# ScalarE scales the normalised rows of the later groups of each layer, with a shift that VectorE makes

## The chip, the cores and the metric

The kernel runs on one core of one Trainium2 chip. The time is device microseconds of the run (median of several runs). The profile is one profiled execution with its own span.

## The reference

Four graph-attention layers over the same 4096 nodes with 64 features and one adjacency matrix. Layer l computes, with `slope` 0.2, 0.01, 0.2, 0.01 and an ELU in layers 0, 2 and 3 (layer 1 adds a bias instead):

```
wh = x @ W
e = leaky_relu((wh @ a_src)[:, None] + (wh @ a_dst)[None, :], slope)
p = softmax(where(adj > 0, e, -big), axis=1)
h = elu(p @ wh)            # layer 1: p @ wh + bias
r = x + h
x = (r - mean(r)) / sqrt(var(r) + 1e-5)     # over the 64 features of each row
```

The adjacency matrix is sparse, with few neighbours for nodes of a high number and many for those of a low one.

## The kernel before, in words

The 4096 rows are 32 tiles of 128 rows (`TILES`), and four tiles make a group (`GROUP`), so there are eight groups. In the first third of the kernel the adjacency matrix is read, and for each tile a list of its neighbours is made (`index`), while layer 0 begins. From then on a tile is worked on in its list form: GpSimd gathers the rows of `wh` of its neighbours from a table in HBM (`table`, one per layer) into `xg`, 128 slots at a time (`gather`, L525, 73 chunks per layer). Tile 0 alone is dense, against all 32 tiles of `wh`. A tile has one or more segments of up to 512 slots.

Each engine has one queue that is written out by hand: `run_round(l, i)` is called for one round after another, and a stage comes into the round that its lag says (`LAG_TILE`, in tiles). Layers 1 to 3 run one tile per round. The stages of a segment are: spread (TensorE, L667 and L669: scores into PSUM), slope (ScalarE, L840), mask (VectorE, L1221), exp (ScalarE, L854), turn (TensorE transposes, L686), copy_turned (ScalarE, L864), aggregate (TensorE, L701).

When a group's last tile is aggregated there follows the group's own part: combine (VectorE, L1238 to L1264, five rounds after the last tile's spread; ScalarE makes the exponential for the ELU, `elow`, L869), center (VectorE, `norm_stats`, one round later, and ScalarE's `estimate_rstd`, L811 and L813), scale (VectorE, `norm_rows`, one round later still), turn_x (TensorE, L561), copy_x (ScalarE, L805), project (TensorE, L571), copy_wh (ScalarE, L797), own (VectorE, L1212) and the write of the group's rows into the next layer's table (SP, L487, from `write_rows`; in the last layer the store, L491).

The order in ScalarE's round is: copy_turned, copy_x, slope, copy_wh, exp, rstd, elu. In VectorE's it is: mask, combine, scale, center, own. In TensorE's: project, turn, aggregate, turn_x, spread. Each engine works in the order of its queue, and waits at semaphores for the others: `x_made` counts groups whose rows are scaled, `rstd_made`, `masked`, `sloped`, `turned_copied` and so on.

The tensors of a group's end (`num`, `res`, `mean_var`, `stat`, `rstd`) have two halves, used in turn.

`GROUP_POS[l][g]` is the group's position in its layer's order. In layers 1 to 3 it is g. In layer 0 the tiles come in the order 0, 20 to 27, 1 to 19, 28 to 31, so the groups end in the order 5, 6, 0, 1, 2, 3, 4, 7. Groups 0 to 4 are the low ones: GpSimd starts the next layer's first 17 gathers (`EARLY`) when these five are written (`low_written`), and the other 56 when all are (`written`).

The rows are scaled in `norm_rows`: three small steps make `stat` (1/std), and then four instructions, one per tile, compute `x = (res - mean) * stat` (L1295), the last of which counts up `x_made`.

Of the kernel before, what the change touches and what calls it, by code (L numbers as in the profile page):

```python
# [24 lines left out]
P = 128  # L25
# [124 lines left out]
def group_n(l, g):  # L150

    return l * GROUPS + GROUP_POS[l][g]


def group_end(l, g):
# [104 lines left out]
def gat_kernel(nc, x_in, adj, adj_t, weights, bias, consts, out):  # L260
    with ExitStack() as ctx:
# [6 lines left out]
        def sem(name):  # L268
            return ctx.enter_context(nc.semaphore(name))
# [81 lines left out]
        stats = sb("stats", [P, GROUP, 6], F32)  # L351
        mean_var = sb("mean_var", [P, 2, GROUP, 2], F32)
        stat = sb("stat", [P, 2, GROUP], F32)
        var = sb("var", [P, 2, GROUP], F32)
        rstd = sb("rstd", [P, 2, GROUP], F32)

# [36 lines left out]
        flag_made = sem("flag_made")  # L393

        x_made = sem("x_made")
        xt_made = sem("xt_made")
        xt_copied = sem("xt_copied")
        wh_made = sem("wh_made")
# [61 lines left out]
        @block.sync  # L460
        def _(sp):
            sp.dma_start(wx[0:F, :, :], weights).then_inc(loaded, 16)
            sp.dma_start(wx[F:2 * F, :, :], weights).then_inc(loaded, 16)
            sp.dma_start(packed[:, :], consts["packed"]).then_inc(loaded, 16)
            sp.dma_start(fix_f[:, :], consts["fix"]).then_inc(loaded, 16)
            sp.dma_start(bit_mask[:, :], consts["bit_mask"]).then_inc(loaded, 16)
            for t, k in enumerate(TILE_AT):
                if t == 2:

                    sp.wait_ge(rows_marked, 1)  # L470
                if t >= 3:

                    sp.wait_ge(mask_made, t - 2)
                sp.dma_start(arena[:, t % 3, :], adj_t[k]).then_inc(adj_loaded[t % 3], 16)
                if t == 0:
                    sp.dma_start(arena[:, 2, :], adj[DENSE * P:(DENSE + 1) * P, :]).then_inc(rows_loaded, 16)
                    sp.dma_start(x[:, :, :], x_in).then_inc(x_loaded, 16)
                    sp.dma_start(slot_row[:, :], consts["slot_row"]).then_inc(slots_loaded, 16)
                    sp.dma_start(bias_sb[:, :], bias.rearrange("(o f) -> o f", o=1).broadcast_to([P, F])).then_inc(
                        slots_loaded, 16)  # L480

            def write_rows(l, g):

                n = group_n(l, g)
                if l < LAYERS - 1:
                    sp.wait_ge(wh_copied, GROUPS + n + 1)
                    sp.dma_start(tab_v[l + 1][:, g, :, :], wh[:, g * GROUP:(g + 1) * GROUP, :]).then_inc(  # L487
                        low_written if g < LOW_GROUPS else written, 16)
                else:
                    sp.wait_ge(x_made, n + 1)  # L490
                    sp.dma_start(out[:, g * GROUP:(g + 1) * GROUP, :],  # L491
                                 x[:, g * GROUP:(g + 1) * GROUP, :]).then_inc(stored, 16)

            for g in GROUP_ORDER[0]:
                write_rows(0, g)
            sp.wait_ge(flag_made, 1)
            over_flag = sp.value_load(flag[0:1, 0:1], min_val=0, max_val=1)
            with sp.If(over_flag == 0):
                for l in range(1, LAYERS):
                    for g in GROUP_ORDER[l]:  # L500
                        write_rows(l, g)
                sp.wait_ge(stored, 16 * GROUPS)
                sp.wait_ge(low_written, 16 * (LAYERS - 1) * LOW_GROUPS)
                sp.wait_ge(written, 16 * (1 + (LAYERS - 1) * (GROUPS - LOW_GROUPS)))
            with sp.Else():

                sp.wait_ge(xt_made, 2 * GROUPS)
                sp.wait_ge(x_made, GROUPS)
                sp.dma_start(x[:, :, :], x_in).then_inc(x_loaded, 16)
                for l in range(LAYERS):  # L510
                    with sp.Fori(0, TILES) as k:

                        sp.wait_ge(d_x, l * TILES + k + 1)
                        sp.dma_start(arena[:, 0, :], adj[bass.ts(k, P), :]).then_inc(d_adj, 16)
                sp.wait_ge(d_x, LAYERS * TILES + 1)
                sp.dma_start(out, x[:, :, :]).then_inc(stored, 16)
                sp.wait_ge(stored, 16)
                sp.wait_ge(low_written, 16 * LOW_GROUPS)
                sp.wait_ge(written, 16 * (1 + GROUPS - LOW_GROUPS))
# [33 lines left out]
        def _(pe):  # L553
# [152 lines left out]
            def run_round(l, i):  # L706

                g = group_of(l, "project", i)
                if g is not None and l < LAYERS - 1:
                    if GROUP_POS[l][g] == 0:  # L710
                        pe.wait_ge(sum_copied, l + 1)
                    project_rows(GROUPS + group_n(l, g), l + 1)
                for q in segs(l, "turn", i):
                    turn(l, q)
                for q in segs(l, "aggregate", i):
                    aggregate(l, q)
                g = group_of(l, "turn_x", i)
                if g is not None and l < LAYERS - 1:
                    if group_n(l, g) == 0:
                        pe.wait_ge(codes_read, LISTED)  # L720
                    pe.wait_ge(x_made, group_n(l, g) + 1)
                    turn_rows(GROUPS + group_n(l, g), g, xt_copied, GROUPS + group_n(l, g))
                for q in segs(l, "spread", i):
                    spread(l, q)
# [69 lines left out]
        def _(sc):  # L794
# [62 lines left out]
            def copy_turned(l, q):  # L857
# [5 lines left out]
                    sc.wait_ge(aggregated, n - ring + 1)  # L863
                nc.scalar.copy(slots(l, n)[:, 0:m * P], turned_ps[turned_bank(n)][:, 0:m * P]).then_inc(turned_copied, 1)  # L864

            def elu_part(l, g):
                h = GROUP_POS[l][g] % 2
                sc.wait_ge(agg_read, group_n(l, g) + 1)
                nc.scalar.activation(elow[:, h, :, :], num[:, h, :, :], ACT.Exp).then_inc(elow_made, 1)  # L869

            def run_round(l, i):
# [16 lines left out]
                g = group_of(l, "elu", i)  # L888
                if g is not None and ELU[l]:
                    elu_part(l, g)  # L890

            done_rounds = 0
            for t in range(BEATS):
# [52 lines left out]
        def _(v):  # L946
# [282 lines left out]
            def combine(l, g):  # L1229
# [25 lines left out]
                t.then_inc(agg_read, 1)  # L1255
                v.wait_ge(agg_read, group_n(l, g) + 1)
                xs = x[:, k0:k0 + GROUP, :]
                if l == BIAS_LAYER:
                    link(nc.vector.tensor_tensor(y, y, bias_sb[:, :].unsqueeze(1).broadcast_to([P, GROUP, F]), ALU.add))
                if ELU[l]:  # L1260
# [25 lines left out]
            def norm_rows(l, g):  # L1286
# [4 lines left out]
                link(nc.vector.tensor_tensor(st, r, r, ALU.mult))  # L1291
                link(nc.vector.tensor_tensor(st, st, var[:, h, :], ALU.mult))
                link(nc.vector.scalar_tensor_tensor(out=st, in0=st, scalar=1.5, in1=r, op0=ALU.add, op1=ALU.mult))
                for j in range(GROUP):
                    t = nc.vector.tensor_scalar(x[:, g * GROUP + j, :], res[:, h, j, :], mean_var[:, h, j, 0:1],  # L1295
                                                st[:, j:j + 1], ALU.subtract, ALU.mult)
# [211 lines left out]
```

## Time and profile before

| | |
|---|---|
| time of the runs (device us) | median 864.14 of 3 (862.48 to 875.75) |
| span of the profiled execution | 608.0 us, 10701 instructions |
| the rest of the time, outside the span | some 256 us of the median |
| mean granted TensorE clock | 0.922 |
| ScalarE busy | 398.5 us in 876 instructions |
| VectorE busy | 366.7 us in 1696 instructions |
| TensorE busy | 394.4 us in 3404 matmuls |

The span runs from the first instruction to the last of the profiled execution. The time of a run holds more than that span; no time of the profiled execution other than its span is given. The busy times are sums over the whole span; the share of an engine differs greatly between the list making (to about 250 us), the beginning of a layer and its end. Layers 1 to 3 take about 100 us each, from about 290 us on.

### The profile page before, as it was taken

To read this page: it belongs to the slowest core of one execution; us is meant where nothing else is said; L and a number is where in the kernel's file an instruction comes from. 1 tells how busy PE (TensorE), PEld (TensorE's weight loads), DVE (VectorE), ACT (ScalarE), POOL (GpSimd) and SP (SyncE) were. 2 spreads that over 40 slices of the span, in tenths; PEclk is the share of its full clock that TensorE was granted. 3 is DMA by queue.
4 is the path that set the end of the run, shared out by engine and by line. 5 is a ranking of instruction groups with operands and counts; after the bars stand their busy time and mean duration, and the time that the engine had idled before them with its cause. 6 is when DMAs were issued, how large, how long until landed. Compare 5 with 4: busy or idle time off the path is not lost.

```text
span 608.0 us, 10701 instructions
## 1 busy us (share of the span) xinstructions
PE 394.4 (65%) x3404; PEld 321.7 (53%) x3404; DVE 366.7 (60%) x1696; ACT 398.5 (66%) x876; POOL 282.3 (46%) x296
## 2 busy tenths in 40 slices
PE   2165454443788548886627997755898876498773
PEld 1154333332576436865416886543787754397552
DVE  2104579965327898898321289854168984218996
ACT  3377876857437776696328588727588863858882
POOL 0000035746024234400777777377777467777710
PEclk9999999999999999999566999959899986899995
DMA  7998999969348861200221122122222113122210
GB/s 300 388 428 333 392 425 403 406 240 295 143 185 273 295 240 15 38 19 26 35 27 27 28 37 46 42 45 30 28 28 46 36 38 46 27 29 37 45 34 25
DMA packets 20547, 84.86 MB, mean 140 GB/s; under 512 B 6083, under 2 KB 11462, under 8 KB 16262
## 3 DMA queue, kind: packets, MB, share of 16 engines
q1 hardware_dynamic: 10102, 73.14, 30.7%
q0 software_dynamic: 9344, 9.89, 12.1%
q10 hardware_dynamic: 1040, 1.08, 0.5%
q8 instruction: 30, 0.49, 0.3%
q14 instruction: 31, 0.25, 0.2%
HBM read 78.72 MB, written 5.37 MB: 138 GB/s over the span
## 4 chain that ended last, share of the span: by engine, by line
DVE 29%; PE 20%; ACT 11%; issue 5%; POOL 3%; DMA 1%; ACTq 0%; DVEq 0%
PE bank L701 9%; DVE num L1252 4%; PE bank L686 4%; DVE arena L1221 3%; DVE x L1295 3%; POOL xg L525 3%; PE bank L669 3%; ACT arena L854 3%; ACT arena L840 3%; DVE stats L1277 3%; DVE lone L1238 2%; PE bank L667 2%; DVE mean_var L1280 2%; ACT arena L864 1%; ACT arena L828 1%
## 5 line engine op out<-in xcount | busy, mean ns | idle before, releaser
L525 POOL DMA_INDIRECT xg<-table,index x292 | 282.1, 966 | 298.2 <-DMA table<-wh 134.9
L828 ACT ACTIVATE arena<-arena,half 128x4096 bf16<-128x4096 int32 x31 | 114.5, 3701 | 18.8 <-DMA arena<-in_adj_t 18.3
L1221 DVE CUSTOM_DVE_ANT_0 arena<-bank,arena 128x256 f32<-128x256 f32 (+3 forms) x123 | 62.8, 521 | 101.3 <-ACT arena L840 101.2
L840 ACT ACTIVATE arena<-bank,sloped_own 128x256 f32<-128x256 f32 (+3 forms) x123 | 67.9, 556 | 53.1 <-PE bank L669 52.1
L701 PE MATMUL bank<-xg,arena 128*128 128x64 f32 x486 | 72.6, 284 | 24.3 <-ACT arena L864 22.6
L701 PEld LDWEIGHTS bank<-xg,arena 128*128 128x128 f32 x486 | 63.6, 197 | 35.3 <-ACT arena L864 31.2
L686 PE MATMUL bank<-packed,arena 128*128 128x128 f32 x339 | 64.7, 312 | 19.1 <-ACT arena L864 16.5
L1018 DVE MAX8 top<-bank 128x8 f32<-128x256 f32 x31 | 13.3, 430 | 84.4 <-PE bank L603 84.3
L669 PE MATMUL bank<-packed,xg 128*128 128x128 f32 x324 | 63.3, 298 | 0.0
L686 PEld LDWEIGHTS bank<-packed,arena 128*128 128x128 f32 x339 | 43.2, 158 | 30.8 <-ACT arena L854 25.6
L864 ACT COPY arena<-bank 128x256 f32<-128x256 f32 (+3 forms) x123 | 53.6, 443 | 6.8 <-PE bank L686 6.2
L667 PE MATMUL bank<-off_row,wall 128*128 128x256 bf16 (+3 forms) x132 | 42.7, 324 | 22.0 <-DVE seg_max L1221 12.3
L854 ACT ACTIVATE arena<-arena,seg_max 128x256 f32<-128x256 f32 (+2 forms) x87 | 47.9, 551 | 4.9 <-DVE seg_max L1221 4.7
L669 PEld LDWEIGHTS bank<-packed,xg 128*128 128x128 f32 x324 | 45.4, 152 | 3.7 <-issue 1.4
L601 PE MATMUL bank<-fix,ones_b 3*128 3x352 bf16 x31 | 14.5, 468 | 45.8 <-ACT arena L828 45.8
L686 PE MATMUL bank<-packed,score 128*128 128x128 f32 x113 | 28.1, 370 | 20.9 <-ACT slots L864 20.4
L840 ACT ACTIVATE score<-bank,sloped_own 128x256 f32<-128x256 f32 (+3 forms) x41 | 22.7, 553 | 28.6 <-PE bank L669 28.4
L571 PE MATMUL bank<-wx_pair,xt 128*128 128x132 f32 x128 | 28.1, 355 | 13.5 <-ACT wh L797 10.1
L603 PEld LDWEIGHTS bank<-packer,arena 128*128 128x128 bf16 x992 | 28.8, 104 | 9.4 <-issue 9.4
L701 PE MATMUL bank<-xg,slots 128*128 128x64 f32 x162 | 28.9, 325 | 6.5 <-DVE num L1252 4.2
L1295 DVE TENSOR_SCALAR x<-res,mean_var,stat 128x64 f32<-128x64 f32 x128 | 32.2, 329 | 1.2
L667 PEld LDWEIGHTS bank<-off_row,wall 128*128 128x128 bf16 x132 | 19.0, 144 | 25.3 <-issue 14.5
(141 smaller groups left out, 765.3 us busy)
## 6 DMA issues: line engine op xcount, KB each, us to landing
arena<-in_adj_t SPq DMA_DIRECT2D x31, 2048.0 KB, 11.0
xg<-table,index POOLq DMA_INDIRECT x292, 2.7
table<-wh SPq DMA_DIRECT2D x24, 132.0 KB, 1.7
arena<-in_adj SPq DMA_DIRECT2D x1, 2048.0 KB, 12.9
table<-wh ACTq DMA_DIRECT2D x1, 1056.0 KB, 25.7
x<-in_x SPq DMA_DIRECT2D x1, 1024.0 KB, 15.0
out_x<-x SPq DMA_DIRECT2D x8, 128.0 KB
packed<-in_c_packed SPq DMA_DIRECT2D x1, 306.0 KB
```

Source lines behind the costliest of these rows:

```text
L525: pool.indirect_dma_start(out=xg[:, c, :], out_offset=None, in_=table[l][0:rows, :], in_offset=bass.IndirectOffsetOnAxis(ap=index[:, c:c + ...
L603: ins = nc.tensor.matmul(codes[:, c * w:(c + 1) * w], masks[:, t % 2, c * P:(c + 1) * P], packer[:, :], start=False, stop=(c == TILES - 1))
L667: nc.tensor.matmul(bank[:, 0:m * P], wall[:, :], marks, start=True, stop=False)
L669: t = nc.tensor.matmul(bank[:, c * P:(c + 1) * P], tcol_wide(terms[:, c1 + c, TCOL:TCOL + 1]), ident[:, :], start=False, stop=(c == m - 1) ...
L686: t = nc.tensor.transpose(turned_ps[turned_bank(n)][:, c * P:(c + 1) * P], scores(l, n)[:, c * P:(c + 1) * P], ident[:, :])
L701: t = nc.tensor.matmul(agg[:, at:at + F], slots(l, n)[:, c * P:(c + 1) * P], wh[:, c0 + c, 0:F] if k == DENSE else xg[:, FIRST[k] + c0 + c ...
L828: nc.scalar.activation(masks[:, t % 2, :], arena[:, t % 3, :], ACT.Sign, bias=half[:, :]).then_inc(mask_made, 1)
L840: nc.scalar.activation(scores(l, n)[:, 0:m * P], score_ps[n % len(score_ps)][:, 0:m * P], ACT.Relu, bias=sloped_own[:, k:k + 1], scale=ALP ...
L854: nc.scalar.activation(s, s, ACT.Exp, bias=least, scale=-1.0, accum_out=seg_sum[:, q:q + 1]).then_inc(exped, 1)
L864: nc.scalar.copy(slots(l, n)[:, 0:m * P], turned_ps[turned_bank(n)][:, 0:m * P]).then_inc(turned_copied, 1)
L1221: nc.vector.tensor_tensor_reduce(out=y, in0=score_ps[n % len(score_ps)][:, 0:m * P], in1=y, scale=-1.0, scalar=-FLOOR, op0=ALU.add, op1=AL ...
L1295: t = nc.vector.tensor_scalar(x[:, g * GROUP + j, :], res[:, h, j, :], mean_var[:, h, j, 0:1], st[:, j:j + 1], ALU.subtract, ALU.mult)
```

## The change

From position 3 on in layers 1 to 3 (five groups of eight) and from position 4 on in layer 0 (four groups), `norm_rows` on VectorE stops after `stat` and makes `shift = -mean * stat` (128x4) in one instruction, counted by `scale_made`. ScalarE then computes `x = Identity(stat * res + shift)`, four ACTIVATEs of 128x64 with scale and bias from columns of `stat` and `shift`, counted by `x_scaled`. It does so at the end of its round of stage "scale", behind that round's copy, slope and exp. TensorE's turn_x and SP's store wait for `x_scaled` in those groups. In combine, VectorE waits for ScalarE to have scaled the group two before, ahead of writing `res`. The other groups are unchanged.

```
+ACT_FROM = [4] + [3] * (LAYERS - 1)
+
+def on_act(l, g):
+    return GROUP_POS[l][g] >= ACT_FROM[l]
+
+def rows_made(l, g, on):
+    n = group_n(l, g) + 1
+    return sum(1 for m in range(LAYERS) for j in range(GROUPS) if group_n(m, j) < n and on_act(m, j) == on)
...
 # SP, write_rows, and TensorE, turn_x
-                    sp.wait_ge(x_made, n + 1)
+                    sp.wait_ge(x_scaled if on_act(l, g) else x_made, rows_made(l, g, on_act(l, g)))
...
-                    pe.wait_ge(x_made, group_n(l, g) + 1)
+                    pe.wait_ge(x_scaled if on_act(l, g) else x_made, rows_made(l, g, on_act(l, g)))
...
 # ScalarE
+            def scale_rows_of(l, g):
+                h = GROUP_POS[l][g] % 2
+                sc.wait_ge(scale_made, rows_made(l, g, True))
+                for j in range(GROUP):
+                    t = nc.scalar.activation(x[:, g * GROUP + j, :], res[:, h, j, :], ACT.Identity,
+                                             bias=shift[:, h, j:j + 1], scale=stat[:, h, j:j + 1])
+                t.then_inc(x_scaled, 1)
...
                 g = group_of(l, "elu", i)
                 if g is not None and ELU[l]:
                     elu_part(l, g)
+                g = group_of(l, "scale", i)
+                if g is not None and on_act(l, g):
+                    scale_rows_of(l, g)
...
 # VectorE, combine
                 xs = x[:, k0:k0 + GROUP, :]
+                n = group_n(l, g)
+                held = [m for m in range(max(0, n - 1)) if on_act(m // GROUPS, GROUP_ORDER[m // GROUPS][m % GROUPS])]
+                if held:
+                    v.wait_ge(x_scaled, len(held))
...
 # VectorE, norm_rows
                 link(nc.vector.scalar_tensor_tensor(out=st, in0=st, scalar=1.5, in1=r, op0=ALU.add, op1=ALU.mult))
+                if on_act(l, g):
+                    nc.vector.scalar_tensor_tensor(out=shift[:, h, :], in0=mean_var[:, h, :, 0], scalar=-1.0, in1=st,
+                                                   op0=ALU.mult, op1=ALU.mult).then_inc(scale_made, 1)
+                    return
                 for j in range(GROUP):
                     t = nc.vector.tensor_scalar(x[:, g * GROUP + j, :], res[:, h, j, :], mean_var[:, h, j, 0:1],
                                                 st[:, j:j + 1], ALU.subtract, ALU.mult)
```

The path for inputs that don't fit the lists (`Else`), which isn't taken here, waits for both counts.

## Rows read from the trace of the kernel before

**Rows 1.** The page, busy time, share of the span and instructions of each engine

```profile
PE 394.4 (65%) x3404; PEld 321.7 (53%) x3404; DVE 366.7 (60%) x1696; ACT 398.5 (66%) x876; POOL 282.3 (46%) x296
```

**Rows 2.** The chain of waits that ended last, by engine

```profile
DVE 29%; PE 20%; ACT 11%; issue 5%; POOL 3%; DMA 1%; ACTq 0%; DVEq 0%
```

**Rows 3.** Windows: one period, layer 2 (length, PE, PEld, DVE, ACT, POOL; clock; DMA)

```profile
482.70:489.60 6.90, 5.76 (x45) 4.44 (x44) 6.36 (x35) 6.05 (x24) 0.12 (x1) 1.00 0.06 20
```

**Rows 4.** Timeline of VectorE, layer 2, two scalings (start, us, engine, line, operation)

```profile
482.74 0.98 DVE L1295 TENSOR_SCALAR x<-res,mean_var,stat 128x64 f32<-128x64 f32 x4
...
483.71 0.42 DVE L1221 CUSTOM_DVE_ANT_0 arena<-bank,arena 128x256 f32<-128x256 f32 x1
...
484.05 0.42 DVE L1221 CUSTOM_DVE_ANT_0 arena<-bank,arena 128x256 f32<-128x256 f32 x1
...
484.40 0.42 DVE L1238 TENSOR_TENSOR lone<-sum_wh,lonely 128x256 f32<-128x256 f32 x1
...
489.62 0.54 DVE L1295 TENSOR_SCALAR x<-res,mean_var,stat 128x64 f32<-128x64 f32 x2
```

**Rows 5.** Timeline of ScalarE over the same scaling

```profile
482.27 0.48 ACT L840 ACTIVATE arena<-bank,sloped_own 128x256 f32<-128x256 f32 x1
482.64 0.51 ACT L854 ACTIVATE arena<-arena,seg_max 128x256 f32<-128x256 f32 x1
483.04 0.20 ACT L854 ACTIVATION_READ_ACCUMULATOR arena<-arena,seg_max 128x1 f32 x1
483.13 0.37 ACT L864 COPY arena<-bank 128x256 f32<-128x256 f32 x1
483.45 0.47 ACT L840 ACTIVATE arena<-bank,sloped_own 128x256 f32<-128x256 f32 x1
484.17 0.51 ACT L854 ACTIVATE arena<-arena,seg_max 128x256 f32<-128x256 f32 x1 [0.25 <-DVE seg_max L1221]
```

**Rows 6.** Groups by line and shape (count, busy us, mean ns; idle before)

```profile
L869 ACT ACTIVATE elow<-num 128x256 f32<-128x256 f32 x24 | 10.0, 416 | 9.4 <-DVE num L1252 9.3
L854 ACT ACTIVATE arena<-arena,seg_max 128x256 f32<-128x256 f32 x60 | 30.5, 508 | 4.7 <-DVE seg_max L1221 4.5
L854 ACT ACTIVATE arena<-arena,seg_max 128x512 f32<-128x512 f32 x9 | 6.4, 711 | 0.0
L816 ACT ACT_TABLE_LOAD x1 | 1.3, 1283 | 0.8 <-PEq L1497 0.8
...
L1293 DVE SCALAR_TENSOR_TENSOR stat<-stat,rstd 128x4 f32<-128x4 f32 x32 | 5.2, 163 | 1.1
```

**Rows 7.** Timelines of ScalarE, TensorE and VectorE, end of layer 2

```profile
495.90 0.63 ACT L864 COPY arena<-bank 128x256 f32<-128x256 f32 x2
...
496.30 1.97 PE L701 MATMUL bank<-xg,arena 128*128 128x64 f32 x8 [1.32 <-ACT arena L864]
...
504.53 0.69 PE L561 MATMUL bank<-packed,x 128*128 128x128 f32 x2 [4.02 <-DVE x L1295]
...
496.62 0.98 DVE L1295 TENSOR_SCALAR x<-res,mean_var,stat 128x64 f32<-128x64 f32 x4
...
498.31 0.47 DVE L1238 TENSOR_TENSOR lone<-sum_wh,lonely 128x256 f32<-128x256 f32 x1 [0.63 <-PE bank L701]
...
503.49 0.98 DVE L1295 TENSOR_SCALAR x<-res,mean_var,stat 128x64 f32<-128x64 f32 x4
```

**Rows 8.** Timelines of TensorE and VectorE, end of layer 0

```profile
283.88 1.10 PE L701 MATMUL bank<-xg,slots 128*128 128x64 f32 x8 [0.56 <-ACT slots L864]
...
284.20 0.98 DVE L1295 TENSOR_SCALAR x<-res,mean_var,stat 128x64 f32<-128x64 f32 x4
...
285.17 0.42 DVE L1238 TENSOR_TENSOR lone<-sum_wh,lonely 128x256 f32<-128x256 f32 x1
```

**Rows 9.** Waits of the whole span (us, times, longest), and GpSimd's timeline

```profile
POOL xg L525 <- issue: 85.9, 282, 0.3
...
489.48 0.94 POOL L525 DMA_INDIRECT xg<-table,index  x1 [9.48 <-DMA table<-wh]
```

More of the change, by code:

```diff
@@ L353, in gat_kernel @@
         stat = sb("stat", [P, 2, GROUP], F32)
+        shift = sb("shift", [P, 2, GROUP], F32)
         var = sb("var", [P, 2, GROUP], F32)
@@ L395, in gat_kernel @@
         x_made = sem("x_made")
+        scale_made = sem("scale_made")
+        x_scaled = sem("x_scaled")
         xt_made = sem("xt_made")
@@ L507, in _ @@
                 sp.wait_ge(xt_made, 2 * GROUPS)
-                sp.wait_ge(x_made, GROUPS)
+                sp.wait_ge(x_made, rows_made(0, GROUP_ORDER[0][-1], False))
+                sp.wait_ge(x_scaled, rows_made(0, GROUP_ORDER[0][-1], True))
                 sp.dma_start(x[:, :, :], x_in).then_inc(x_loaded, 16)
```

## The prediction

> **What bounds the kernel now.** I read four views, in this order. The page's engine totals: no engine passes 66% of the span [rows 1], so a total can't say what an engine's relief is worth. The chain of waits: VectorE has 29% of it, TensorE 20%, ScalarE 11% [rows 2]; it is a chain that hops between engines. Third, the windows over one group period (four tiles) late in a layer: in 6.9 us VectorE is busy for 6.36 and ScalarE for 6.05, TensorE for 5.76 at the full clock [rows 3]. Both engines that the change touches are nearly full there, and that is where the change acts. Fourth, the timelines of the two engines across one norm_rows, which decide.
>
> Number the groups p0 to p7 by their position in the layer's order. A group's combine, center and scale fall in rounds that I call A, B and C; the next one is D, and then the next group's A. In layer 2 the scaling of p4 starts at 482.74, that of p5 at 489.62: a period of 6.88 us [rows 4]. VectorE: three small statistics steps, four scalings (0.98 us together), the mask of D at 483.71, the mask of A at 484.05, the combine from 484.40, and from there to the next scaling there is no gap on it but some tenths around ScalarE's rstd. ScalarE: exponential of C until 483.13, copy of D at 483.13, slope of D 483.45 to 483.92, then it waits 0.25 us for a mask [rows 5]. The mask of A reads what the slope of D wrote. So VectorE and ScalarE turn in one loop: slope of D, mask of A, combine, statistics (VectorE), rstd (ScalarE), scaling (VectorE). Between the end of the slope of D (483.92) and the mask of A that uses it (484.05) there is a slack of 0.13 us, of which the hand-over needs about 0.03. That slack is all that ScalarE may lose there.
>
> **What the change does to that loop.** VectorE loses four scalings per moved group (0.98 us) and gains the shift, of the form of L1293, 163 ns [rows 6], with 0.03 us to the next: 0.79 us off VectorE. 19 groups move: p4 to p7 of layer 0, p3 to p7 of the other three. The shift ends at about 482.91, before ScalarE's queue is free at 483.13, so scale_made makes it wait for nothing in rounds with tiles. But the four ACTIVATEs stand at the end of round C, ahead of the copy, the slope and the exponential of D in ScalarE's queue. Call their time in that queue S. The slope of D ends at 483.92 + S, the mask of A starts at 483.95 + S instead of 484.05. TensorE's aggregate and turn_x wait for the same copy, its spread stands behind them in order; all shift by S together, none gets later than that. From the mask of A to the next scaling everything is as before, so the period grows by S - 0.10. The 0.79 us that VectorE saves are spent by it waiting for the slope of D.
>
> **The price S.** The trace has no ACTIVATE of 128x64 with a scale and a bias from columns. The nearest rows: 128x256 from SBUF without a column operand (elow) 416 ns, with a bias column (exponential) 508; 128x512 of the latter 711 [rows 6]. That is 0.80 ns per column of the tile and about 92 ns for the operand. At 64 columns: 508 - 192 x 0.80 = 354 ns with one column operand, and 446 with two if the second costs what the first did. Successive ACTIVATEs overlap by some 0.10 us (slope at 482.27 for 0.48, exponential at 482.64 [rows 5], which is 0.11), so 0.346 each and S = 1.38. Bounds: second operand free, 4 x 0.254 = 1.02; both free (elow's row), 4 x 0.162 = 0.65; no overlap, 4 x 0.446 = 1.78. I take 1.38, since the exponential's row differs from elow's by just such an operand; that its accumulated output costs the 92 ns in place of the column is the way to the lower values.
>
> The row of the exponential shows a bias column's price; the Trainium skill, in "ScalarE: Activation LUTs", section "What ACT_TABLE_LOAD costs", says that an ACTIVATE takes 186 ns + 0.833 per element, 93 more for each column operand, and that neighbours overlap by 93. The rows at 256 agree (416 and 508 against 399 and 492); no row here shows the second operand. An estimate by that page is S = 1.33. The same page's "Rules for kernel authors" would keep adds and multiplies on VectorE, which speaks against the change.
>
> **The sum, group by group.**
> - p3 to p5 of layers 1 to 3 and p4, p5 of layer 0, eleven groups: S - 0.10 each. The period is 6.8 to 7.0 us in all of them and the same loop stands in each.
> - p6. No tiles are left after it, but two copies stand behind its rstd, at 495.90, and now the scaling lies between them: the second copy can't start before 496.62 + 0.17 + 0.03 + S. It takes 0.36, then TensorE's last aggregate (half of eight matmuls in 1.97 us: 0.99), then p7's combine at 498.24 + S with hand-overs, against 498.31 [rows 7]: S - 0.07. So in layers 2 and 3. In layers 0 and 1 the eight take 1.10 and the combine starts right behind VectorE's scaling: 284.20 + 0.20 + S + 0.36 + 0.03 + 0.55 + 0.04 against 285.17 [rows 8]: S + 0.21. Together 4S + 0.28.
> - p7 of layers 1 to 3 has nothing behind it; its own latency counts. The shift takes the place of the scaling at 503.49, and TensorE's turn starts at 503.49 + 0.20 + S + 0.14 against 504.53 [rows 7]: S - 0.70. Three times: 3S - 2.10. In layer 3 the store stands for the turn. p7 of layer 0 is not on the path: what starts layer 1's tiles is GpSimd's early gathers, and they wait for the low groups alone, of which p6 is the last.
>
> Sum: 18S - 2.92 us. With S = 1.38 it is +21.9.
>
> **What costs nothing.** The wait for x_scaled ahead of res in combine is for the group two before, a whole period old; VectorE queues behind it, but it has passed. SP waits for x_scaled in layer 3 in place of x_made; only p7's store ends the kernel, counted above. The writes of layers 1 and 2 follow the copies of wh, later by what the groups are. GpSimd is the queue to check: its 17 early gathers of layer 3 start at 489.48 and, at 0.94 us and 0.30 of issue each [rows 9], end at about 510.6; the last write of layer 2 lands near 509 (an estimate: p7's turn at 504.53 [rows 7], and 4.7 us for its copy, projection, second copy and write). p3 and p4 delay the start by 2.6, all five delay the last write by 5.9 us; it would stand idle for some 1.8 us and be 4.4 late, less than those who use its rows. If that cover is gone, up to 2 us per layer come on top.
>
> Against the profiled execution: span 608.0 to 629.9 us. The time of the runs holds some 256 us around the span, which the change leaves alone; so 864.14 + 21.9 = 886.0.
>
> **The rivals.**
> 1. The ACTIVATEs are cheaper than their rows: S between 0.65 and 1.12. At S = 1.02 the sum is 15.4, 879.6 us; at 0.65 it is 8.8, 872.9. For it: the exponential also accumulates, which may be what the 92 ns buy. Against: its read of the accumulator is an instruction of its own [rows 5]. 2% is 17.3 us, which S = 1.12 gives; this is also about what a measurement can tell from no change.
> 2. The other side: the relief counts, since VectorE has no gap. ScalarE's own waits (0.25 us ahead of the exponential of D and the one ahead of rstd) would have to take the ACTIVATEs, which needs the slope of D to be early; then each of the eleven periods loses 0.79 us: -8.7, 855.4 us. It decides at the slack in the queue: S below 0.10, or a copy and slope of D that stand ahead of the scaling. The order of the queue and every row of ScalarE (none under 0.2 us) speak against it.
> 3. TensorE loses its clock. A new gap of S stands in every period. At the half level (1.2 GHz) the eight aggregates take 1.97 us instead of 1.10 [rows 7, 8]. With 5.76 us of matmuls per period [rows 3] it would be near 10.3, over the new period of 8.2: 2.1 us x 11 more, +23, 909 us. Against: the clock stood at 1.00 there, and the share of busy time falls only from 0.83 to 0.70.
> 4. Identity calls for another activation table. One load takes 1.28 us [rows 6], two per group, 19 groups: +49 on top, 935 us. For it: the kernel before uses no Identity in its trace. Against: copies, Relu, Sign, Exp and Ln run on one load. The Trainium skill, same page, "Table sets: the hidden batching unit", has identity in every set; no run shows it yet.
>
> **How the numbers follow.** Forecast (S 1.12 to 1.78): 0.57. Rival 1: 0.31. Rival 2: 0.05, rival 3: 0.04, rival 4: 0.01, and 0.02 for a gain that I don't see. The forecast's own range is 881 to 893, from 17.3 to 29.1 us. To hold 8 in 10 the range reaches down over most of rival 1, to 870, and up to 893. Slower by over 2%: 0.57 + 0.05, 0.62. Within 2%: rival 1 and most of rival 2, 0.35. Faster by over 2%: 0.03.
>
> **What would show it.** In the profile after: p4 to p5 of layer 2 at 8.2 us instead of 6.88; ScalarE's four ACTIVATEs at 0.35 us spacing right behind the exponential of C, and the slope of D behind them; VectorE idle for over a microsecond ahead of a mask, released by the slope, once per moved group; p0 to p2 unchanged. The forecast is wrong if the spacing is near 0.2, if the period stays at 6.9, or if VectorE's mask doesn't wait.

## The result and the profile after

The changed kernel takes 884.22 us (median of 5 runs, 878.45 to 897.81), the kernel before 862.48 beside it (5 runs, 859.62 to 875.75). The ratio is 1.0237, 95% interval 1.0188 to 1.0286; it leaves out the runs that lie over 1.5% above their kernel's fastest, which are the two near 897 us and the one of 875.75. So the change makes the kernel slower, and whether by more than 2% isn't decided. A warning on that interval: the kernel before, run against itself in a later job (run 1 below), gave 1.0094, interval 1.0019 to 1.0169. A few runs of this kernel can mislead by 1%. Its median was 876.99, 875.66 and 873.41 us in the three later jobs, where it is 862.48 here, and the changed kernel was timed in this one job only. So the readings below come from the traces wherever they can, and the ratios only frame them.

The page of the changed kernel, its span and totals:

```profile
span 876.6 us, 10746 instructions
PE 424.6 (48%) x3404; PEld 347.7 (40%) x3404; DVE 353.4 (40%) x1639; ACT 425.0 (48%) x952; POOL 277.0 (32%) x296
```

Against [rows 1] VectorE has lost 57 instructions (76 scalings gone, 19 shifts come) and 13 us, and ScalarE has gained 76 instructions and 26.5 us. But the span is 876.6 us, where 608.0 and a cost of some 20 would give about 630. Some 256 us that no row of the first profile shows are inside the execution here. Run 1 shows that this is so in the kernel before too: a timed run is only about 1.9 us longer than its own span, and the execution of 608.0 us was of another kind than the timed ones. So run 1's trace, and not that of the 608.0 us execution, is what the trace after has to be read against.

The four ACTIVATEs by their line (count, least/median/greatest ns):

```profile
L890 ACT ACTIVATE x<-res,shift,stat x76: 424/431/442, 305.4 to 873.5; 128x64 f32<-128x64 f32 x76
```

ScalarE's timeline over the scaling of p4 in layer 2, and the next one (start, us; the numbers answer to [rows 5]):

```profile
669.23 0.20 ACT L873 ACTIVATION_READ_ACCUMULATOR arena<-arena,seg_max 128x1 f32 x1
669.32 1.43 ACT L890 ACTIVATE x<-res,shift,stat 128x64 f32<-128x64 f32 x4
670.65 0.35 ACT L883 COPY arena<-bank 128x256 f32<-128x256 f32 x1
670.90 0.47 ACT L859 ACTIVATE arena<-bank,sloped_own 128x256 f32<-128x256 f32 x1
...
677.37 0.76 ACT L890 ACTIVATE x<-res,shift,stat 128x64 f32<-128x64 f32 x2
```

VectorE over the same stretch (it answers to [rows 4]):

```profile
668.93 0.16 DVE L1330 SCALAR_TENSOR_TENSOR shift<-mean_var,stat 128x4 f32<-128x4 f32 x1
669.01 0.16 DVE L1243 TENSOR_SCALAR sloped_own<-wh 128x4 f32<-128x4 f32 x1
669.08 0.42 DVE L1252 CUSTOM_DVE_ANT_0 arena<-bank,arena 128x256 f32<-128x256 f32 x1
...
671.41 0.42 DVE L1252 CUSTOM_DVE_ANT_0 arena<-bank,arena 128x256 f32<-128x256 f32 x1 [1.90 <-ACT arena L859]
671.76 0.42 DVE L1269 TENSOR_TENSOR lone<-sum_wh,lonely 128x256 f32<-128x256 f32 x1
```

Read the two together. ScalarE starts the scaling at 669.32, right behind the exponential of round C; the copy of D comes 1.33 us later, the slope of D ends at 671.37, and VectorE's mask of A starts at 671.41, after 1.90 us of idleness that the slope ends. Before, that mask stood back to back with the one ahead of it. The period from this scaling to the next is 8.05 us, where [rows 4] have 6.88 and the prediction had 8.2.

The same stretch by windows (length; PE, PEld, DVE, ACT, POOL busy; granted clock; DMA), and one of layer 3:

```profile
669.40:677.40 8.00, 5.52 (x41) 4.47 (x40) 5.58 (x32) 7.22 (x28) 0.54 (x1) 0.97 0.05 18
...
839.10:847.60 8.50, 7.13 (x36) 6.35 (x34) 5.63 (x32) 6.82 (x25) 0.00 (x0) 0.60 0.04 15
```

VectorE's 6.36 us of [rows 3] are 5.58, as it should be, in a longer period. In layer 3 TensorE's granted clock is 0.60, between its levels of 2.4 and 1.2 GHz (a mix of both in the window), where the kernel before has 1.00; these periods take 8.5 us instead of 8.05. The clock falls at about 840.7, where TensorE takes up work after the second of two idle gaps, 1.12 us (to 838.33) and 1.13 (to 840.77). A gap of over a microsecond is no sign by itself: run 1 has one of 1.12 us per period in layer 3 at 1.00, and the window of layer 2 above has one of 1.14 at 0.97.

### The profile page after: what moved, and what is told of

The parts are those of the page before. It is cut to its first block, busy times and chain, and to the rows that moved or that the text cites. A ratio compares the mean times of both kernels' runs of the same rounds, so it can differ in the third digit from the quotient of the medians.

```text
span 876.6 us, 10746 instructions
## 1 busy us (share of the span) xinstructions
PE 424.6 (48%) x3404; PEld 347.7 (40%) x3404; DVE 353.4 (40%) x1639; ACT 425.0 (48%) x952; POOL 277.0 (32%) x296
## 2 busy tenths in 40 slices
DMA packets 20548, 84.86 MB, mean 97 GB/s; under 512 B 6084, under 2 KB 11463, under 8 KB 16263
## 4 chain that ended last, share of the span: by engine, by line
another core or an unknown queue 19%; PE 17%; DVE 14%; ACT 13%; issue 11%; ACTq 0%; DVEq 0%
PE bank L720 7%; ACT arena L873 3%; PE bank L688 3%; PE bank L705 3%; ACT x L890 3%; ACT arena L859 2%; DVE num L1283 2%; ACT arena L883 2%; PE bank L686 2%; DVE stats L1312 2%; DVE arena L1252 1%; DVE lone L1269 1%; DVE mean_var L1315 1%; ACT arena L847 1%
## 5 line engine op out<-in xcount | busy, mean ns | idle before, releaser
L544 POOL DMA_INDIRECT xg<-table,index x292 | 276.8, 948 | 506.5 <-DMA table<-wh 306.4
L705 PE MATMUL bank<-packed,arena 128*128 128x128 f32 x339 | 71.5, 334 | 115.0 <-issue 80.1
L720 PE MATMUL bank<-xg,arena 128*128 128x64 f32 x486 | 80.5, 304 | 47.0 <-ACT arena L883 42.7
L705 PEld LDWEIGHTS bank<-packed,arena 128*128 128x128 f32 x339 | 49.6, 173 | 124.5 <-issue 103.4
L720 PEld LDWEIGHTS bank<-xg,arena 128*128 128x128 f32 x486 | 71.9, 219 | 59.4 <-ACT arena L883 53.7
L686 PE MATMUL bank<-off_row,wall 128*128 128x256 bf16 (+3 forms) x132 | 46.2, 350 | 81.5 <-issue 70.8
L688 PE MATMUL bank<-packed,xg 128*128 128x128 f32 x324 | 70.2, 322 | 0.0
L688 PEld LDWEIGHTS bank<-packed,xg 128*128 128x128 f32 x324 | 50.2, 166 | 4.6 <-issue 2.3
L622 PE MATMUL bank<-packer,arena 128*128 128x11 bf16 x992 | 34.4, 173 | 16.0 <-issue 16.0
L622 PEld LDWEIGHTS bank<-packer,arena 128*128 128x128 bf16 x992 | 30.3, 105 | 26.1 <-issue 26.0
L686 PE MATMUL bank<-off_dense,wall 128*128 128x512 bf16 x32 | 16.8, 526 | 39.9 <-DVE seg_max L1252 22.2
```

The source lines that it names most:

```text
L544: pool.indirect_dma_start(out=xg[:, c, :], out_offset=None, in_=table[l][0:rows, :], in_offset=bass.IndirectOffsetOnAxis(ap=index[:, c:c + ...
L622: ins = nc.tensor.matmul(codes[:, c * w:(c + 1) * w], masks[:, t % 2, c * P:(c + 1) * P], packer[:, :], start=False, stop=(c == TILES - 1))
L686: nc.tensor.matmul(bank[:, 0:m * P], wall[:, :], marks, start=True, stop=False)
L688: t = nc.tensor.matmul(bank[:, c * P:(c + 1) * P], tcol_wide(terms[:, c1 + c, TCOL:TCOL + 1]), ident[:, :], start=False, stop=(c == m - 1) ...
L705: t = nc.tensor.transpose(turned_ps[turned_bank(n)][:, c * P:(c + 1) * P], scores(l, n)[:, c * P:(c + 1) * P], ident[:, :])
L720: t = nc.tensor.matmul(agg[:, at:at + F], slots(l, n)[:, c * P:(c + 1) * P], wh[:, c0 + c, 0:F] if k == DENSE else xg[:, FIRST[k] + c0 + c ...
```

## The experiments

Ten runs follow; run 1 is the kernel before, the other nine have an edit each. S is the time that the four scalings take in ScalarE's queue; rounds A to D and groups p0 to p7 are those of the prediction. A "stretch" below is the time from the end of p3's scaling in layer 0 to the end of p7's in layer 3, from the starts of L1295 and L890 (or their like) and their lengths in one profile. It leaves out the list making at the start, whose length differs by some 25 us from run to run. Where a period is said to be "by the statistics", it goes from the start of VectorE's last statistics step (`stat<-stat,rstd`, L1293 or its like) of one group to that of the next. This step stands in every group of every kernel, while the scaling itself starts later once it is moved.

**1. The kernel before, once more.** No edit.

> The kernel before, once more, for its profile in the state in which the timed runs are. The profile shown ahead of the prediction has a span of 608.0 us where the runs take 862; the profile of the changed kernel has 876.6 of 878.5. Theory A (the missing 256 us are stretches inside the execution in which engines stand idle, the same in both kernels): span about 860, idle stretches at the ends and beginnings of layers 1 to 3, late group periods of 6.9 us as in the first profile. Theory B (they lie outside the span in the kernel before and the change brought the stretches in): span near 608 again.

Measured: span 883.7 us. Theory A holds. Of the 275.7 us between the two spans, 218 lie in the stretch and 45 ahead of layer 0's first scaling. Behind layer 0, ScalarE, VectorE and TensorE stand idle together for over 2 us at a time once in the 608.0 us execution (7.8 us), and 27 times here, 182 us in all. The idle stretches stand where the timeline of GpSimd shows gathers one behind the other. In layer 1's dense part (ScalarE, VectorE and TensorE, with GpSimd's row):

```profile
388.63 0.94 POOL L525 DMA_INDIRECT xg<-table,index  x1 [0.30 <-issue]
...
390.43 0.69 ACT L840 ACTIVATE arena<-bank,sloped_own 128x512 f32<-128x512 f32 x1 [13.31 <-remote]
391.15 0.69 DVE L1221 CUSTOM_DVE_ANT_0 arena<-bank,arena 128x512 f32<-128x512 f32 x1 [13.30 <-ACT arena L840]
...
392.38 1.06 PE L669 MATMUL bank<-packed,wh 128*128 128x128 f32 x4
...
404.43 0.69 ACT L840 ACTIVATE arena<-bank,sloped_own 128x512 f32<-128x512 f32 x1 [13.31 <-remote]
```

TensorE is done at 393.44 and ScalarE's slope of its scores starts at 404.43. In the 11.0 us between, no engine but GpSimd has an instruction; where GpSimd is quiet such a hand-over takes about 0.03. The late periods are as in the first profile. A window of layer 2:

```profile
676.50:683.40 6.90, 5.76 (x45) 4.45 (x45) 6.38 (x35) 6.05 (x23) 0.00 (x0) 1.00 0.06 20
```

**7 and 8. Both kernels without the gathers of layers 1 to 3.** One gather per layer is left, and the layers compute with the rows of layer 0.

```
-                    for c in EARLY:
-                        gather(l, TILES_OF_CHUNK[c][0], c, LOW * P)
...
-                    for c in range(NCH):
-                        if c not in EARLY:
-                            gather(l, TILES_OF_CHUNK[c][0], c)
+                    gather(l, 1, FIRST[1])
...
-                    pe.wait_ge(gathered[k], 16 * OWN[k] * (l + 1))
+                    pe.wait_ge(gathered[k], 16 * (OWN[k] + (l if k == 1 else 0)))
```

> The kernel before with one gather in each of layers 1 to 3 in place of 73: the rows gathered in layer 0 are used again, so these layers compute something else; all the rest of the work is the same. Theory A (the idle stretches of 5 to 13 us come with GpSimd's gathers, since they lie exactly where GpSimd is busy): they are gone from the layers 1 to 3, and the time falls from 862 to about 600. Rival (they have another cause, such as the code after the branch being fetched): they stay, over 800 us.

> The changed kernel with the same cut. If theory A holds there is no idle stretch to hide behind in layers 1 to 3, and the whole sum should show against the kernel before with the cut: 18 x 1.33 - 2.92 = 21 us, of which layer 0 has 4, each of the others 5.6. Rival (the sum overrates p6 and p7 by itself, not because of the idle stretches): 14 us.

Measured: medians 640.97 us (before) and 668.02 (changed), four runs each; the fastest runs 629.61 and 657.13, 27.5 apart. The idle stretches are gone from layers 1 to 3 (theory A; those that are left lie in the list making, with layer 0's gathers). The stretch is 329.7 us in the one and 357.1 in the other, so the change costs 27.3 us when nothing hides it: 6.9 in layer 0, 7.7, 6.1 and 6.7 in the others. That is more than the 21 of the sum. The rest goes with a lower clock, as in the windows of the two kernels over p4 of layer 1, changed kernel first:

```profile
423.50:431.80 8.30, 6.88 (x42) 6.04 (x42) 5.57 (x33) 7.20 (x27) 0.00 (x0) 0.79 0.06 19
```

```profile
414.50:421.40 6.90, 5.69 (x45) 4.49 (x45) 6.38 (x35) 5.82 (x22) 0.00 (x0) 1.00 0.07 22
```

and in two periods of run 8 by the statistics, p3 to p4 of layer 1 and of layer 2:

```profile
413.57:422.43 8.86, 7.73 (x41) 7.31 (x42) 5.71 (x31) 6.99 (x25) 0.00 (x0) 0.61 0.04 14
521.19:529.24 8.05, 5.56 (x43) 4.48 (x44) 5.63 (x32) 7.27 (x27) 0.00 (x0) 1.00 0.06 19
```

The granted clock parts these periods. The changed kernel and runs 5 and 8 have 29 periods behind a moved inner group that no idle stretch falls into. In ten of them the clock stands at 0.97 or 1.00, and each of the ten takes 8.04 or 8.05 us, within 0.07 of the prediction's rule. In the other 19 the clock is between 0.50 and 0.80, and they take 8.22 to 9.10. In run 9 below (shorter scalings, 7.68 us at the full clock) two periods are long at 1.00 and 0.98, 8.09 and 8.13 us; both follow directly on one with a lowered clock (0.80 and 0.62). In run 8 the seven of that kind are 4.6 us over 8.05 together, which is most of the 6.3 that the sum lacks; p6 is 1.6 over its terms. Without the change (the first profile, runs 1 and 7) 28 of the 31 such periods have 0.96 or more.

**2. The same four ACTIVATEs behind the slope of round D.**

```
                 for q in segs(l, "slope", i):
                     slope(l, q)
+                g = group_of(l, "scale", i - 1)
+                if g is not None and on_act(l, g):
+                    scale_rows_of(l, g)
...
-                g = group_of(l, "scale", i)
-                if g is not None and on_act(l, g):
-                    scale_rows_of(l, g)
```

> The same four ACTIVATEs, moved in ScalarE's queue from the end of round C to behind the copy and the slope of round D; nothing else changes. Queue theory (they cost because the slope of D, and with it VectorE's mask of A, stands behind them): the mask of A is not delayed any more; what remains is ScalarE's own fullness, 6.05 us + 1.33 of work in a period, so late periods of about 7.4 in layers with an ELU (6.9 in layer 1) in place of 8.05 to 8.25; in all some 12 to 15 us less than the changed kernel, ratio to before 1.005 to 1.01. Rival (what costs is that ScalarE has more work at all, or the longer hand-over VectorE to ScalarE to TensorE): periods stay above 8, ratio 1.02.

Measured: ratio 1.0139 (1.0009 to 1.0269), stretch 569.2 us against 575.2 of the changed kernel and 559.3 of the kernel before. ScalarE, layer 2, p5:

```profile
683.37 0.37 ACT L883 COPY arena<-bank 128x256 f32<-128x256 f32 x1
683.69 0.47 ACT L859 ACTIVATE arena<-bank,sloped_own 128x256 f32<-128x256 f32 x1
684.06 1.42 ACT L890 ACTIVATE x<-res,shift,stat 128x64 f32<-128x64 f32 x4
685.39 0.50 ACT L873 ACTIVATE arena<-arena,seg_max 128x256 f32<-128x256 f32 x1
```

and VectorE's mask of A:

```profile
684.20 0.42 DVE L1252 CUSTOM_DVE_ANT_0 arena<-bank,arena 128x256 f32<-128x256 f32 x1 [0.59 <-ACT arena L859]
```

The mask starts 0.04 us behind the slope, under the scalings instead of behind them. Layer 1, which has no ELU, has periods of 6.84 and 6.83 us, no more than before; in layers 2 and 3 p4 to p5 takes 7.67 and 7.44. By the statistics, which don't move with the scaling, the periods behind moved inner groups are 7.67 and 7.68 in layer 0, 6.83 twice in layer 1, 8.45 and 8.13 in layer 2, and 7.32, 8.08 and 7.45 in layer 3. The longest two of layers 2 and 3 stand at a clock of 0.63 (8.45) and 0.50 (8.08); the 8.13 follows the first of them. Where there is no ELU the queue theory is right: the order alone takes 1.2 us per period away, with the same work on ScalarE. In the layers with an ELU it takes 0.4 to 1.4 us away in layers 0 and 3 and nothing in layer 2, where the periods were 8.24 and 8.04, so there the rival, that ScalarE has more work at all, isn't refuted. The total fell by 6 us in the stretch, less than the 12 to 15 expected; the ratio, whose interval is wide, can't decide between its two expectations.

**3. The scalings made twice** (first into a spare tile).

```
+                for j in range(GROUP):
+                    nc.scalar.activation(spare[:, j, :], res[:, h, j, :], ACT.Identity,
+                                         bias=shift[:, h, j:j + 1], scale=stat[:, h, j:j + 1])
                 for j in range(GROUP):
                     t = nc.scalar.activation(x[:, g * GROUP + j, :], res[:, h, j, :], ACT.Identity,
```

> ScalarE makes each of the four scalings twice, once into a spare tile that nobody reads. S goes from 1.33 to 2.66 us per group. Queue theory by the sum 18 S - 2.92: 45 us over before in place of 21, so 24 us more than the changed kernel, ratio to before about 1.052; late periods of 9.4 to 9.6 us. Rival (ScalarE's time is partly covered): less than 12 us more.

Measured: ratio 1.0634 (1.0434 to 1.0834), stretch 604.6 us, 45.3 over the kernel before, against 45.0 by the sum. One period of layer 1, p4 to p5 (ScalarE):

```profile
512.65 1.43 ACT L894 ACTIVATE x<-res,shift,stat 128x64 f32<-128x64 f32 x4
520.70 1.43 ACT L891 ACTIVATE spare<-res,shift,stat 128x64 f32<-128x64 f32 x4
522.02 1.43 ACT L894 ACTIVATE x<-res,shift,stat 128x64 f32<-128x64 f32 x4
```

It is 9.37 us, so nothing of ScalarE's second 1.33 us was covered. That the whole stretch meets the sum so closely is partly chance: 5.0 us of the 45.3 lie between p7 of layer 0 and p0 of layer 1, where the other profiles with idle stretches differ by 3.9 us among themselves (130.3 to 134.2), whatever the edit.

**4. Plain copies in place of the scalings.** The normalisation of the moved groups is left out.

```
-                    t = nc.scalar.activation(x[:, g * GROUP + j, :], res[:, h, j, :], ACT.Identity,
-                                             bias=shift[:, h, j:j + 1], scale=stat[:, h, j:j + 1])
+                    t = nc.scalar.copy(x[:, g * GROUP + j, :], res[:, h, j, :])
```

> ScalarE copies the four tiles of res to x without scale and shift: the normalisation of the moved groups is left out, with all waits and the same four instructions in number and size. It takes both column operands away. By the row of elow 0.26 us each, 0.16 apart, S = 0.65: sum 8.8 us over before, ratio 1.010, late periods of 7.4 us. Rival (the hand-over, not S, is what costs): as the changed kernel, 1.02.

**9. The shift from its column, the scale a constant.** The division by the deviation is left out in the moved groups.

```
                     t = nc.scalar.activation(x[:, g * GROUP + j, :], res[:, h, j, :], ACT.Identity,
-                                             bias=shift[:, h, j:j + 1], scale=stat[:, h, j:j + 1])
+                                             bias=shift[:, h, j:j + 1], scale=1.0)
```

> The changed kernel with the shift from its column but a scale of 1.0 as a constant, so the moved groups are not divided by their deviation. It prices the second column operand. If each column operand costs about 92 ns, as the prediction took it: 0.34 us each where the changed kernel has 0.43, 0.24 apart, S = 0.98, late periods of 6.88 + 0.98 - 0.10 = 7.76 us at the full clock. Rival (the second operand is free): 0.43 us and 8.05 as in the changed kernel.

Measured, the forms of the two (mean ns), plain copies first:

```profile
L890 ACT COPY x<-res 128x64 f32<-128x64 f32 x76 | 12.8, 242 | 4.6 <-DVE shift L1329 4.4 <-issue 0.2
```

```profile
L890 ACT ACTIVATE x<-res,shift 128x64 f32<-128x64 f32 x76 | 20.1, 337 | 5.0 <-DVE shift L1330 4.4 <-issue 0.6
```

So 242, 337 and 431 ns for no, one and two column operands: each costs 94 to 95 ns, the second like the first, and they start 0.144, 0.24 and 0.333 us apart. Four such starts make S = 0.58, 0.96 and 1.33. The periods p4 to p5 of layer 1 follow them; from the starts, the copies first and then the one column:

```profile
509.61 0.67 ACT L890 COPY x<-res 128x64 f32<-128x64 f32 x4
516.93 0.67 ACT L890 COPY x<-res 128x64 f32<-128x64 f32 x4
```

```profile
510.49 1.05 ACT L890 ACTIVATE x<-res,shift 128x64 f32<-128x64 f32 x4
518.17 1.05 ACT L890 ACTIVATE x<-res,shift 128x64 f32<-128x64 f32 x4
```

| | S | period of layer 1, p4 to p5 | 6.88 + S - 0.10 | eleven periods over run 1 | 11 S - 0.76 | stretch over run 1 | 18 S - 2.92 |
|---|---|---|---|---|---|---|---|
| plain copies | 0.58 | 7.32 | 7.36 | 8.4 | 5.6 | 5.9 | 7.5 |
| one column | 0.96 | 7.68 | 7.74 | 13.7 | 9.8 | 15.3 | 14.4 |
| changed kernel | 1.33 | 8.05 | 8.11 | 17.0 | 13.9 | 15.9 | 21.0 |
| scaled twice | 2.66 | 9.37 | 9.44 | 33.9 | 28.5 | 45.3 | 45.0 |

This period obeys the prediction's rule to 0.07 us over more than a factor of four in S, always 0.04 to 0.07 below it. It is the period where the rule fits best: p3 to p4 of the same layer takes 7.51, 8.12, 8.22 and 10.19 us by the statistics, up to 0.8 over the rule, at clocks of 0.67 to 0.79. The eleven periods are those behind moved groups into which no idle stretch falls (p4 to p6 of layer 0, p3 and p4 of layers 1 and 2, p3 to p6 of layer 3), by the statistics, and 11 S - 0.76 is the prediction's sum for them alone. They lie 2.8 to 5.4 us above it. The stretches scatter by several us round their sum, since each is one profile and holds idle stretches too. The ratio of run 4 is 1.0124 (0.9936 to 1.0313), which decides nothing; run 9 was timed once, at 897.90 us.

**5. Only the eleven inner groups; 6. only p6 and p7.**

```
-    return GROUP_POS[l][g] >= ACT_FROM[l]
+    return ACT_FROM[l] <= GROUP_POS[l][g] <= 5      # run 5
+    return GROUP_POS[l][g] >= 6                     # run 6
```

> Only the eleven groups that are followed by more tiles go to ScalarE (p3 to p5 of layers 1 to 3, p4 and p5 of layer 0); p6 and p7 stay on VectorE. By the sum with S = 1.33: 11 x 1.23 = 13.5 us over the kernel before; by the anchors of the two profiles that show the idle stretches (layers 1 and 2 lost nothing at p6 and p7) about the same cost as the changed kernel in layers 1 and 2, some 3.5 and 2.9 us from p2 to p5. Queue theory: late periods of 8.1 to 8.5 us for the moved groups, ratio about 1.016. Rival (the long latency of ScalarE at the very end of a layer is what costs): under 5 us, ratio 1.005.

> Only p6 and p7 of every layer go to ScalarE. By the sum with S = 1.33: p6 4 x 1.33 + 0.28, p7 3 x 0.63, 7.5 us. Idle theory (at the end of layers 1 and 2 every engine stands idle for over 10 us at a time anyway, and hides what p6 and p7 lose): 1.3 in layer 3's p6, 0.6 in its p7, 1.5 in layer 0, 3.5 us, ratio 1.004; from p5 to p7 of layers 1 and 2 the same as in the kernel before, 30.3 to 30.7 us.

Measured: run 5, ratio 1.0125 (0.9893 to 1.0358), stretch 573.5 us, 14.2 over the kernel before, against 13.5 by the sum; periods of 8.05 to 8.6 us by the statistics behind the inner groups of layers 0 and 3 and behind p3 and p4 of layers 1 and 2. Behind p5 of layers 1 and 2 it shows no cost: from p5's to p7's statistics it takes 30.2 and 30.7 us, as in run 1 (30.3 and 30.7).

Run 6, ratio 1.0163 (0.9942 to 1.0384), stretch 570.1 us, 10.8 over, where 3.5 was expected. Of those, 2.3 are in layer 0 and 2.0 in layer 3, from p5 on, and 1.4 in layers 1 and 2. The other 5.0 lie ahead of any moved group (1.7) and between the layers (3.3), in parts that differ by as much between the profiles whatever the edit. From p5 to p7 it takes 31.1 and 31.3 us in layers 1 and 2, against 30.3 and 30.7 in run 1 and 29.7 and 30.4 in the changed kernel. So p6 and p7 cost at most a microsecond there; without gathers (run 8 against 7) the same stretches grow by 3.1 and 2.5. How the idleness hides it is to be seen at p6 of layer 2, changed kernel, ScalarE:

```profile
691.35 1.43 ACT L890 ACTIVATE x<-res,shift,stat 128x64 f32<-128x64 f32 x4
700.89 0.37 ACT L883 COPY arena<-bank 128x256 f32<-128x256 f32 x1 [8.10 <-remote]
```

and the same copy of run 1, where no scaling stands ahead of it:

```profile
714.19 0.37 ACT L864 COPY arena<-bank 128x256 f32<-128x256 f32 x1 [9.48 <-remote]
```

The copy comes 11.65 us after the start of the rstd's second step in the one (689.24) and 10.97 in the other (703.22): ScalarE's 1.33 us fill idle time of 9.48.

**10. Half of the scalings, behind the slope.** Two tiles on VectorE, two on ScalarE, whose start is that of run 2. TensorE's turn and SP's store wait for both counts.

```
-                for j in range(GROUP):
+                for j in range(GROUP // 2, GROUP):          # ScalarE
...
+                    for j in range(GROUP // 2):             # VectorE, behind shift
+                        t = nc.vector.tensor_scalar(x[:, g * GROUP + j, :], res[:, h, j, :], mean_var[:, h, j, 0:1],
+                                                    st[:, j:j + 1], ALU.subtract, ALU.mult)
+                    t.then_inc(x_half, 1)
```

> Two of the four scalings stay on VectorE, ScalarE makes the other two, behind the copy and the slope of round D: S = 0.76, and VectorE is rid of 0.49 us for 0.17 of shift. Queue theory: the mask of A starts as soon as the slope of D has ended, 0.1 us earlier than before, but the exponential for the ELU comes 0.3 to 0.4 us later and eats it; late periods of 6.8 to 7.0 us in every layer, no loss and no gain against the kernel before, ratio 0.995 to 1.005. Rival (VectorE's relief counts once the queue is in order): periods of 6.5, 4 us less than before.

Measured: ratio 0.9984 (0.9898 to 1.0069). The period p4 to p5 of layer 3 from VectorE's scalings:

```profile
847.85 0.53 DVE L1339 TENSOR_SCALAR x<-res,mean_var,stat 128x64 f32<-128x64 f32 x2
854.64 0.53 DVE L1339 TENSOR_SCALAR x<-res,mean_var,stat 128x64 f32<-128x64 f32 x2
```

6.79 us, against 6.81 of the kernel before in run 1; in layer 1 it is 6.79 against 6.88. The other periods behind moved inner groups take 6.78 to 7.04 by the statistics, and one of layer 2 takes 7.48, at a clock of 0.77. No loss and no gain that the ratio could show, as the queue theory had it.

## Why the prediction was right

The median of 884.22 us lies 1.8 from the 886.0 forecast, and the rise of 21.7 us next to the 21.9 of the sum. So close a match is luck: the medians of the kernel before in the three later jobs lie 11 to 15 us higher than the one that the 21.7 are counted from, and the single profiles give 15.9, in which two errors of the sum partly cancel (see the end of this section). What the runs bear out is the mechanism; the steps one by one:

- **The loop and its slack: right.** That the slope of D stands behind the scaling and the mask of A behind the slope is in the rows after, the idleness of 1.90 us with its releaser among them. Runs 3, 4 and 9 show the rule (period + S - 0.10) over the whole range of S where the clock isn't lowered, and run 2 shows that it is the place in the queue that costs in layer 1: with the slope ahead, its period is back at 6.84. In layers with an ELU, run 2 shows that only in part.
- **The price S: right, a little high.** 431 ns measured against 446, 0.333 us apart against 0.346, S = 1.33 against 1.38. The estimate by the page of the Trainium skill ("ScalarE: Activation LUTs", section "What ACT_TABLE_LOAD costs") was 1.33. Its 93 ns per column operand stand beside 95 and 94 here.
- **The second operand, and with it rival 1:** taken from a single pair of rows, the exponential and elow; runs 4 and 9 bear it out (95 and 94 ns), so S wasn't in the range of rival 1, and the accumulated output was not what the 92 ns bought.
- **p6 and p7: right without the idle stretches, hidden in layers 1 and 2 with them, and p5 too.** Run 8 has them in full. Run 6 shows at most 1 us for p6 and p7 there, run 5 nothing for p5, and the changed kernel nothing for all three (29.8 and 30.6 us from p5's to p7's statistics, against 30.3 and 30.7).
- **"The time of the runs holds some 256 us around the span": wrong.** They are inside the execution, mostly in idle stretches while GpSimd gathers. It changed the forecast little, because p3 and p4 of layers 1 and 2 and the moved groups of layers 0 and 3 fall where GpSimd is mostly quiet. The cover at GpSimd that the prediction worried about isn't there in this kind of execution either: between its 17th and 18th gather of layer 3 GpSimd waits 15.7 us in run 1 and 16.4 in the changed kernel, and from p7's statistics to the next layer's p0 it takes 109.5 and 110.4 us in run 1, 110.0 and 109.5 in the changed kernel, so its extra 2 us per layer don't show. (Its 5.9 us of delay at the last write are 5.8 by its own terms.)
- **Rival 3, the clock: ruled too unlikely, and priced wrongly.** It came true in part. The clock falls in six of the changed kernel's nine inner periods outside the idle stretches (0.60 in the window of layer 3, 1.00 before), but TensorE doesn't become the bound: those periods are 0.2 to 1.0 us over the 8.04 or 8.05 of the others, not 2.1. That its matmuls stretch mostly into gaps that stood there already would explain the low price, but that is argued. No run held the clock up, so it isn't shown either that the lower clock makes these periods long, and not the other way round.
- **Rival 4, a table load:** none; the changed kernel's trace has the same single load, at 0.8 us, as the kernel before. The Trainium skill, "ScalarE: Activation LUTs", section "Table sets: the hidden batching unit", has identity in every set, and the trace agrees. **Rival 2, a gain:** none, even in run 10 where the queue is in order and VectorE has less to do.

Taken together, in executions of the timed kind the single profiles give 15.9 us where the medians give 21.7. Two errors of the sum act against each other: p5, p6 and p7 of layers 1 and 2, 6.5 us of its 21.0, are hidden, and the eleven other inner and p6 periods cost 17.0 us in place of 13.9, most of it where the clock is lower. Which of the two figures is nearer to the truth can't be settled with runs that scatter by 10 us.

## What to carry to other kernels

When two engines take turns in a loop, relief of the fuller one is worth nothing if the work lands in the other's queue ahead of what the first waits for: ask what stands behind the new instruction, and what slack that has (here 0.1 us). Before averaging over periods, sort them by the granted clock: here that parted 8.05 us from 8.2 to 9.1 in one and the same loop. The price of an instruction on ScalarE depends on its operands as much as on its width, 0.14 to 0.33 us of queue for the same 128x64. And where the span and the timed runs differ by a third, profile the kernel again before trusting what its idle time covers.

## What was unexpected of the hardware

The kernel had executions of two kinds: one of 608.0 us of span with hardly an idle stretch, and those of all its timed runs, 859 to 889 us, in which hand-overs between engines take up to 13 us as long as GpSimd issues its indirect gathers, at an exact beat of 14.0 us in the dense part (two of ScalarE's slopes are at 390.43 and 404.43). The two kinds move the same 20547 packets and 84.86 MB. Leaving out the gathers of three layers took 235 us off the median (875.66 to 640.97). So the gathers are needed for the long hand-overs, but they don't suffice: the 608.0 us execution had them all. GpSimd itself keeps its pace of 1.25 us per gather meanwhile. The trace names "remote" or an unknown queue as the releaser; what is held up, and why the first execution was spared, these runs don't tell.
